# Eight heads in one row: reordering the steps of the later attentions in a fused fp32 transformer kernel

## The reference

```python
h = shift_token(x)                       # half of the columns come from the token before
q, k, v = split(h @ wqkv)                # 8 heads, 64 wide
q = l2norm(q) * qs; k = l2norm(k) * ksc
q, k = rotary_xpos(q, k)
# windows of 128 queries see their own 128 keys and the 128 before
sim = bq @ bk.T;  attn = softmax(where(mask, -max, sim));  o = attn @ bv
x = x + o @ wo
h = layernorm(shift_token(x)) * lg + lb
a, g = split(h @ w1 + b1);  x = x + (a * gelu(g)) @ w2 + b2
```

## Time and profile before

| | us |
|---|---|
| median of 3 runs | 1907.88 |
| lowest, highest | 1906.34, 1909.03 |
| the profiled execution | 1905.08 |
| its span in the trace | 1903.4 |
| PE busy | 1822.6 (96%) |
| DVE busy | 1580.5 (83%) |
| ACT busy | 1190.0 (63%) |
| POOL busy | 1090.9 (57%) |
| the two later attentions | about 625 to 1058 and 1268 to 1700 |

### The profile page before, as it was taken

One profiled execution on the slowest core, in us unless ns is written; L12 is line 12 of the kernel. 1 busy time (PEld: TensorE's weight loads), 2 busy tenths in 40 slices (PEclk: granted clock), 3 DMA queues, 4 the chain that ended last, 5 costly groups with the idle time before them and its releaser, 6 DMA issues. The chain is left out here.

```text
span 1903.4 us, 43278 instructions
## 1 busy us (share of the span) xinstructions
PE 1822.6 (96%) x15168; PEld 1529.0 (80%) x15168; DVE 1580.5 (83%) x3853; ACT 1190.0 (63%) x3084; POOL 1090.9 (57%) x1040
## 2 busy tenths in 40 slices
PE   6999999989999899999999999989999999989997
PEld 4777777768998788888887888878888888878886
DVE  6888888877988899999998566779999999966776
ACT  5787777764445577777776433347777777753332
POOL 3555444443434677777765355457777777634443
PEclk9999999999999999999999999989999999999999
DMA  2110111003241211111112333231111111122221
GB/s 100 32 34 30 52 42 33 21 24 106 77 121 47 97 41 51 41 49 48 43 46 65 120 110 109 93 116 36 50 50 40 51 42 49 35 81 67 77 77 34
DMA packets 139667, 116.01 MB, mean 61 GB/s; under 512 B 10440, under 2 KB 138704, under 8 KB 138704
## 3 DMA queue, kind: packets, MB, share of 16 engines
q1 hardware_dynamic: 139472, 113.53, 19.4%
HBM read 75.74 MB, written 37.75 MB: 60 GB/s over the span
## 5 line engine op out<-in xcount | busy, mean ns | idle before, releaser
L1715 ACT ACTIVATE b_probs<-masked,neg_max 128x256 f32<-128x256 f32 (+1 forms) x512 | 249.9, 498 | 8.3 <-DVE neg_max L1257 8.2
L542 PE MATMUL psum<-wa_hi,b_h_hi 128*128 128x512 f32 (+1 forms) x576 | 234.9, 408 | 0.2
L1257 DVE CUSTOM_DVE_ANT_0 masked<-psum,mask 128x256 f32<-128x256 f32 (+1 forms) x512 | 182.2, 412 | 43.4 <-PE psum L818 34.4
L544 PE MATMUL psum<-wa_hi,b_h_lo 128*128 128x512 f32 (+1 forms) x576 | 215.3, 374 | 0.0
L543 PE MATMUL psum<-wa_lo,b_h_hi 128*128 128x512 f32 (+1 forms) x576 | 215.1, 373 | 0.0
L542 PE MATMUL psum<-g_h_hi,wm_hi 128*128 128x512 f32 (+1 forms) x480 | 190.4, 397 | 6.2 <-POOL g_h_lo L1978 4.6
L1926 POOL TENSOR_TENSOR g_in<-g_in,minus_half 128x16 f32<-128x16 f32 x64 | 188.9, 2952 | 0.4 <-DVE g_in L1217 0.4
L543 PE MATMUL psum<-g_h_lo,wm_hi 128*128 128x512 f32 (+1 forms) x480 | 188.9, 394 | 0.0
L544 PE MATMUL psum<-g_h_hi,wm_lo 128*128 128x512 f32 (+1 forms) x480 | 188.8, 393 | 0.0
L1808 ACT ACTIVATE gate<-psum,vec_b 128x512 f32<-128x512 f32 x96 | 66.0, 687 | 168.6 <-PE psum L544 168.4
L542 PE MATMUL psum<-wm_hi,u_hi 128*128 128x256 f32 x576 | 165.6, 287 | 0.1
(11 more groups left out here) (161 smaller groups left out, 5778.3 us busy)
## 6 DMA issues: line engine op xcount, KB each, us to landing
x_mid<-y_out SPq DMA_DIRECT2D x96, 128.0 KB, 1.7
rope_in<-in_rope SPq DMA_DIRECT2D x64, 128.0 KB, 2.2
x_res<-x_state SPq DMA_DIRECT2D x64, 128.0 KB, 2.2
g_in<-x_mid SPq DMA_DIRECT2D x32, 256.0 KB, 3.7
g_old<-x_state SPq DMA_DIRECT2D x16, 512.0 KB, 4.1
out_x<-g_fin SPq DMA_DIRECT2D x15, 512.0 KB, 3.0
w_raw<-in_w_mlp_b SPq DMA_DIRECT2D x2, 2154.0 KB, 9.2
x_in<-in_x SPq DMA_DIRECT2D x32, 128.0 KB, 2.1
```

The source lines that it names most:

```text
L542: nc.tensor.matmul(out, a_hi, b_hi, start=first, stop=False)
L544: return nc.tensor.matmul(out, a_lo, b_hi, start=False, stop=last)
L1257: ins = nc.vector.tensor_tensor_reduce(out[:, at], src[:, at], (mask if now else mask0)[:, at], -1.0, BIG, ALU.add, ALU.min, neg_max[:, r, ...
L1715: ins = nc.scalar.activation(out, src, ACT.Exp, bias=neg_max[:, r, k:k + 1], scale=-1.0, accum_out=row_sum[:, n % 2, 4 * r + k:4 * r + k + 1])
```

## The change

In the later attentions a step now handles a chunk as a whole. Scores of heads 0 to 3 go to banks 4 and 5, those of heads 4 to 7 to banks 6 and 7, one right after the other; then come both halves of the values of the chunk before, and its spread. The transposed probabilities go back into the banks of their own scores. The output projection leaves bank 1 for bank 4 (6 and 5 at two places near the end). The order on every engine is written anew, `invert_sums` and `widen_inverse` belong to the step of their own chunk, and the openings of the MLP behind are placed anew in the last steps. Counts and sizes of operations stay. The diff is cut to the new order and the waits; the old order is in the code above, and the smaller edits are the bank numbers that go with the new places.

```diff
-def b_spread(n):
-
-    return 4 if n == NCH - 1 else 1
+def b_out(n):
+
+    return {NCH - 3: 6, NCH - 1: 5}.get(n, 4)


...


 def b_steps():
...
+                if n > 3:
+                    pe.wait_ge(S["r_copied"], g0 + n - 3)
...
+                    pe.wait_ge(S["h_hi"], g0 + n + 1)
+                    pe.wait_ge(S["h_lo"], g0 + n + 1)
...
-                if n + r > 0:
-                    pe.wait_ge(S["max_ready"], i)
+                if n > 0:
+                    pe.wait_ge(S["pt_act"], i - 1)
+                    pe.wait_ge(S["pt_dve"], i - 1)
+                if n > 2 and r == 0:
+                    pe.wait_ge(S["y_ready"], g0 + n - 2)
...
-                        out = bank[4 + b][:, j * 256:j * 256 + 256].rearrange("p (a k) -> p a k", a=2)
+                        out = bank[4 + 2 * r + b][:, j * 256:j * 256 + 256].rearrange("p (a k) -> p a k", a=2)
...
-                if n + r > 0:
-                    pe.wait_ge(S["pt_act"], i)
-                    pe.wait_ge(S["pt_dve"], i)
+                if n == NCH - 1 and r == 1:
+                    pe.wait_ge(S["y_ready"], g0 + NCH - 2)
...
-                        mm = nc.tensor.transpose(bank[6 + k // 2][:, at:at + P], b_probs[:, r, k, half, :], ident[:])
+                        mm = nc.tensor.transpose(bank[4 + 2 * r + k // 2][:, at:at + P], b_probs[:, r, k, half, :], ident[:])
...
                 pe.wait_ge(S["inv_wide"], g0 + n + 1)
-                pe.wait_ge(S["h_lo"], g0 + min(n + 5, NCH))
+                pe.wait_ge(S["v_copied"], g0 + min(n + 3, NCH))
                 if n == NCH - 1:
+                    pe.wait_ge(S["r_copied"], g0 + n)
+                for t in range(4):
+                    mm = nc.tensor.transpose(W2[:, t * P:t * P + P], b_inv_wide[:, t * P:t * P + P], ident[:])
+                mm.then_inc(S["inv_spread"], 1)
+
+            def out_project(n):
+                if n == NCH - 3:
                     pe.wait_ge(S["max_ready"], 2 * (g0 + NCH))
-                elif n > 0:
-                    pe.wait_ge(S["y_ready"], g0 + n)
-                out = bank[b_spread(n)]
-                for t in range(4):
-                    mm = nc.tensor.transpose(out[:, t * P:t * P + P], b_inv_wide[:, t * P:t * P + P], ident[:])
-                mm.then_inc(S["inv_spread"], 1)
-
-            def out_project(n):
-                pe.wait_ge(S["h_lo"], g0 + min(n + 6, NCH))
-                pe.wait_ge(S["v_copied"], g0 + min(n + 4, NCH))
+                elif n == NCH - 1:
+                    pe.wait_ge(S["pt_dve"], 2 * (g0 + NCH) - 1)
+                else:
+                    pe.wait_ge(S["pt_act"], 2 * (g0 + min(n + 2, NCH - 1)) + 1)
                 pe.wait_ge(S["o_hi"], g0 + n + 1)
                 pe.wait_ge(S["o_lo"], g0 + n + 1)
                 for k in range(c.KO):
-                    mm = product3(W2[:, 0:D], b_o_hi[:, k * P:k * P + P], b_o_lo[:, k * P:k * P + P],
+                    mm = product3(bank[b_out(n)][:, 0:D], b_o_hi[:, k * P:k * P + P], b_o_lo[:, k * P:k * P + P],
                                   wo_hi[:, k, :], wo_lo[:, k, :], k == 0, k == c.KO - 1)
...
+            for s in b_steps():
                 if b_chunk(s):
-                    scores(s, r)
...
+                    scores(s, 0)
+                    scores(s, 1)
+                if b_chunk(s - 1):
+                    values(s - 1, 0)
+                    values(s - 1, 1)
                     spread_inverse(s - 1)
...
+                if s == NCH:
+                    pe_mlp(pe, MLP_B, MB, layer, opening=0)
+                if s == NCH + 1:
+                    pe.wait_ge(S["pt_act"], 2 * (g0 + NCH))
+                    pe.wait_ge(S["pt_dve"], 2 * (g0 + NCH))
+                    pe_mlp(pe, MLP_B, MB, layer, opening=1)
+                if s == NCH - 1:
+                    out_project(s - 2)
+                if b_chunk(s + 2) and s + 2 > 1:
+                    project_k(s + 2)
+                if b_chunk(s):
+                    transpose_probs(s, 0)
+                if b_chunk(s + 2) and s + 2 > 1:
+                    project_q(s + 2)
+                if b_chunk(s + 3) and s + 3 > 1:
+                    transpose_x(s + 3)
+                if s == NCH - 1:
                     pe.wait_ge(S["kt_copied"], g0 + NCH)
                     pe.wait_ge(S["qt_copied"], g0 + NCH)
                     pe_mlp(pe, MLP_B, MB, layer, opening="z")
-                if (s, r) == (NCH, 1):
-                    pe_mlp(pe, MLP_B, MB, layer, opening=0)
-                if (s, r) == (NCH + 1, 0):
-                    pe.wait_ge(S["pt_act"], 2 * (g0 + NCH))
-                    pe.wait_ge(S["pt_dve"], 2 * (g0 + NCH))
-                    pe_mlp(pe, MLP_B, MB, layer, opening=1)
+                if b_chunk(s):
+                    transpose_probs(s, 1)
+                if b_chunk(s + 1):
+                    transpose_rotated(s + 1, 1)
+                    transpose_rotated(s + 1, 0)
+                if b_chunk(s - 2) and s != NCH - 1:
+                    out_project(s - 2)
+                if b_chunk(s + 2):
+                    project_v(s + 2)
...
+            for s in b_steps():
+                if s == NCH - 1:
+                    dve_mlp(v, MLP_B, MB, layer, opening=0)
+                if b_chunk(s):
+                    maxima(s, 0)
+                    maxima(s, 1)
+                if s == NCH - 1:
+                    dve_mlp(v, MLP_B, MB, layer, opening=1)
+                if b_chunk(s + 1) and s + 1 > 1:
+                    rotate_q(s + 1)
+                if b_chunk(s - 1):
+                    scale_o(s - 1)
+                if s == NCH - 1:
                     add_residual(s - 2)
...
+                    copy_probs(s, 0)
+                if s == NCH - 1:
+                    dve_mlp(v, MLP_B, MB, layer, opening=2)
+                if b_chunk(s + 1) and s + 1 > 0:
+                    scale_rotated(s + 1)
+                if s == 0:
+                    dve_mlp(v, *mlp_behind(layer), None if layer == 0 else layer - 1, opening="finish")
+                if b_chunk(s + 2) and s + 2 > 1:
+                    norms(s + 2, 1)
+                if b_chunk(s):
+                    copy_probs(s, 1)
+                if b_chunk(s + 2) and s + 2 > 1:
+                    norms(s + 2, 0)
+                if b_chunk(s):
+                    invert_sums(s)
+                if s == NCH - 1:
+                    dve_mlp(v, MLP_B, MB, layer, opening=3)
+                if b_chunk(s + 3) and s + 3 > 2:
+                    h_low(s + 3)
+                if b_chunk(s + 1):
+                    k_t_low(s + 1)
+                    q_t_low(s + 1)
+                if b_chunk(s - 2) and s != NCH - 1:
+                    add_residual(s - 2)
...
-                    if b_chunk(s - 1):
-                        copy_probs(s - 1, 1)
-                    if 4 <= s < 4 + 2 * SPLIT and s % 2 == 0:
-                        split_high(a, w_raw, wm_hi, wm_loaded, wm_hi_done, MLP_B.WCOLS, (s - 4) // 2, layer + 1)
-                else:
...
+            for s in b_steps():
+                if b_chunk(s + 1):
+                    copy_v(s + 1)
+                if b_chunk(s):
+                    exponentials(s, 0)
+                if b_chunk(s - 1):
+                    copy_spread(s - 1)
+                if b_chunk(s):
+                    exponentials(s, 1)
+                if b_chunk(s + 2) and s + 2 > 1:
+                    copy_qk(s + 2, 1)
+                    copy_qk(s + 2, 0)
+                if b_chunk(s):
+                    copy_probs(s, 0)
+                if b_chunk(s + 3) and s + 3 > 1:
+                    h_high(s + 3)
+                if b_chunk(s):
+                    copy_probs(s, 1)
+                if b_chunk(s + 1):
+                    k_t_high(s + 1)
+                    q_t_high(s + 1)
+                if s == NCH - 1:
+                    act_mlp(a, MLP_B, MB, layer, opening=True)
+                if b_chunk(s - 1):
+                    o_high(s - 1)
+                if 4 <= s < 4 + 2 * SPLIT and s % 2 == 0:
+                    split_high(a, w_raw, wm_hi, wm_loaded, wm_hi_done, MLP_B.WCOLS, (s - 4) // 2, layer + 1)
...
-                        tables(s + 2)
-                    if 4 <= s < 4 + 2 * SPLIT and s % 2 == 0:
-                        split_low(pool, nc.gpsimd, w_raw, wm_lo, wm_hi, wm_hi_done, wm_split, MLP_B.WCOLS, (s - 4) // 2, layer + 1)
-                    if b_chunk(s + 2) and s + 2 > 1:
-                        rotate_k(s + 2)
...
+                if b_chunk(s - 2):
+                    o_low(s - 2)
+                if s == NCH - 1:
+                    pool_mlp(pool, MLP_B, MB, layer, opening=0)
+                if s == NCH:
+                    pool_mlp(pool, MLP_B, MB, layer, opening=1)
+                if b_chunk(s + 1) and s + 1 > 1:
+                    inverse_norms(s + 1)
+                if b_chunk(s + 2) and s + 2 > 1:
+                    tables(s + 2)
+                if 4 <= s < 4 + 2 * SPLIT and s % 2 == 0:
```

(5 more changed lines are left out.)

123 lines of the change are left out of this document (11 added, 112 removed).

## The result

The changed kernel takes 1966.13 us (median of 4 runs, 1965.09 to 1967.71) against 1907.11 (1904.71 to 1909.03) for the kernel before: ratio 1.0311, 95% interval 1.0293 to 1.0329, **59 us slower**. I had forecast 1951. The profiled execution took 1967.71 us with a span of 1966.0, which is 62.6 more than the span of before. Where they went shows in the view of busy time by stretch. The borders are PE's first scores product of chunk 0, 4, 20 and 30, the first product of the MLP, and chunk 0 of the next layer. Columns: stretch, its length, busy PE, PEld, DVE, ACT, POOL, PEclk, DMA share, GB/s.

The account below looks back on a forecast made before the run. PE was taken to set the 13.2 us period, DVE 1 us behind. Per layer -4.3 plain chunks, +28.8 pairs, -0.8 chunk 16, +2.3 start, -4.5 end: +21.5, +43 for two layers, median 1951 us, range 1918 to 1974.

Parts of the forecast that it names:

- the mechanism named: Even steps 4 to 18: POOL's split_low, ahead of rotate_k and widen_inverse, waits 5 to 6 us for ACT's now last split_high.
- The pairs: Even step with a weight piece plus the next odd step: 30.0 instead of 26.4 us, +3.6, 8 pairs per layer, +28.8.
- The odd step: Step after a weight piece, from 12.8 to 30.0: PE waits for the widened inverse, DVE later for the inverse norms.
- The 1.3 for rotate_q's meetings with POOL: Odd step: rotate_q on DVE meets POOL's rotate_k, widen and o_low; +1.3 us, between 0 and 1.6.
- Plain chunk: Chunks without a weight piece: 12.85 us, PE bound at 12.8 with DVE at 12.7; -0.36 each, 12 per layer, -4.3.
- The end: From scores(30, 0) to the first MLP product, 29.8 us before: about -4.5 per layer, bounds -7 and 0.
- The start: First steps of a layer lose overlap, PE waiting for DVE's whole step: +2.3 per layer, bounds 0 and 4.
- The reciprocal's price: Reciprocal of the sums on DVE, now beside POOL's rotate_k: between nothing and 0.7 us per chunk, taken as nothing.
- Rival 1: POOL's slack swallows the wait for split_high, all chunks bound by PE: 1882 us in all, chance 0.10.
- Rival 2: No rotate_q meeting, tables not in the way, ACT one slot earlier: 27.6 per pair, 1912 us, chance 0.10.
- rival 3: DVE bounds plain chunks, through the reciprocal or a tensor_scalar held by rotate_k: 13.4 instead of 12.85, 1964 us, chance 0.14.
- Rival 4: POOL's power operation blocks rotate_q in plain chunks: 12 lose 1.4 us each, +34, 1985 us, chance 0.02.

Follow-up runs that it names:

- experiment 1: Changed kernel with ScalarE's weight piece (split_high) at the head of its step, behind copy_v, instead of last: 1903.86 us, 0.9985 of the kernel before.
- experiment 2: Changed kernel with POOL's split_low behind widen_inverse instead of ahead of rotate_k, split_high left last on ScalarE: 1891.66 us, 0.9919 of the kernel before.
- experiment 3: Kernel before the change, old order, with only split_high moved to the end of ScalarE's second half step: 2032.19 us, ratio 1.0659.
- experiment 9: Kernel of experiment 8 with VectorE's scaling of the values done twice in every chunk: 1913.89 us, 1.0026 of the kernel before.
- Experiment 4: Changed kernel with the MLP's first loads issued ahead of the store of chunk 28 on SyncE: 1957.39 us, 1.0265 of the kernel before.
- experiment 8: Changed kernel with split_low behind widen_inverse, MLP loads ahead of chunk 28's store, and MLP statistics behind chunk 31's maxima: 1873.53 us, 0.9832 of the kernel before.

## Why the prediction was right or wrong

- **Slower, in the range, by the mechanism named.** POOL waits 47.4 us for wm_hi, 8 times, longest 6.4 (forecast 5 to 6 each); the widenings alternate between 12.2 and 17.6. The pairs cost +28.8 in the first layer's stretch and +26.8 in the second's, where the forecast had 28.8 - 0.8 = 28.0. Experiments 1, 2 and 3 show the cause from both sides: two ways to take the wait away give back 62 and 74.5 us, and the late piece alone makes the old kernel 126 us slower.
- **The odd step: the right length, in part by luck.** From 757.30 to 774.48 it takes 17.2 us, as forecast (30.0 - 12.8), but by other parts. The stretch behind PE's wait, with the columns of the first view, and VectorE's next two operations:

```profile
763.80:767.12 3.32, 3.32 (x11) 2.75 (x12) 2.46 (x3) 2.17 (x8) 3.32 (x2) 0.53 0.00 0
```

```profile
768.19 0.69 DVE L1363 COPY b_pt<-psum 128x512 f32<-128x512 f32 x1 [1.89 <-PE psum L839]
...
768.80 1.53 DVE L1240 TENSOR_TENSOR g_in<-g_in 128x512 f32<-128x512 f32 x2
```

The 4.6 us over a plain step are 3.0 at the spread (forecast 2.2), 1.4 in the spread and the K projection behind it, which PE did at a granted clock of 0.53 (0.77 and 2.55 us instead of 0.42 and 1.48), and 0.25 where scale_rotated met POOL's tables (1.53 instead of 1.28). The forecast let the inverse norms come last. They were there at 768.47, and VectorE still worked on the copy of probabilities, for which it had stood 1.89 us waiting for PE; only in two of the eight pairs did it wait for the norms (2.1 us in all). The lower clock had no term in the forecast. The 1.3 for rotate_q's meetings with POOL are there (its addition at 764.05 takes 1.64 instead of 0.69), but they end as the spread's copy arrives, for which VectorE had to wait anyway. Both chains ended within 0.3 us of each other, so that by an estimate from these rows full clock alone would give back only these 0.3.

- **Plain chunk: right sign, undersized.** Forecast 12.85 (-0.36), measured 12.56 (-0.64). PE's parts on its timeline: two score groups 1.62 (936.50 to 938.12, forecast 1.59), both values groups 1.90 (to 940.02, forecast 2.06), spread 0.42 (to 940.44, forecast 0.49), V projection into scores 1.48 (947.58 to 949.06, forecast 1.57). With these and smaller differences in the rest the sum of 12.8 was 0.24 too long, and 0.05 were added for nothing in case VectorE came close. The claim that VectorE is 0.1 us below PE was right: experiment 9 measures 0.14 to 0.2. VectorE's loop is thus 12.3 to 12.4, not the 12.7 that I worked out; both loops were overestimated by nearly the same.
- **The end: wrong sign, the step that failed.** The forecast said about -4.5 per layer, "with one round per chunk instead of two", and "SP's queue is unchanged". The queue's order is unchanged, but its store of chunk 28 waits for a residual add that the change moves to the end of VectorE's step, and the loads stand behind it. And VectorE's statistics, which stood behind a first group of maxima, stand ahead of all of them. Measured +5.9 and +3.5 in the two layers, and +2.0 and +1.9 behind the border, where two output projections now lie instead of one. Experiment 4 takes 6.3 of the first layer's end away, experiment 8 8.6, and then it is shorter than before the change. The granted clock has a share in it that no run separates: the same 229 matmul records kept PE busy for 22.96 us at 0.86, and for 20.05 at 1.00.
- **The number** was 15 short, mostly for this reason. For the profiled execution the forecast was +43 and the result +62.6. Both ends together are 18.3 above the forecast and the stretches behind them 3.8; the larger gain of the ten plain chunks takes 5.5 back, and the rest are small terms. This makes 19.6; the medians show 15, since the profiled execution after the change was 1.6 above its median, and I had counted with 2.8 below.
- **The start:** +2.2 and +3.6 against +2.3.
- **The reciprocal's price** is nothing: 186/196/199 ns as shortest, median and longest of 64. The Trainium skill (SBUF — State Buffer, "Who interferes with whom") does not list it among those that take the shared port; the trace agrees.
- **Rival 1** (1882) named what would be had without the wait; experiment 2 with 1891.66 comes near it. Its ends are 35.6 and 33.9 us, 18 more than forecast, and its shorter plain chunks take a part of that back. As a forecast it was wrong: ACT's piece came at the place in its queue that I gave. **Rival 2** (27.6 per pair) and **rival 3** (13.4 per plain chunk) are refuted by 29.7 and 12.56. **Rival 4** is refuted: VectorE's product at 940.28 ran undisturbed under POOL's power, and the plain chunk has no 1.4 us more.

## What to carry to other kernels

When an engine gets a new order, look for the instruction that becomes last, and at every queue in which somebody waits for it: the waiting instruction's own place decides what stands behind it. Moving the consumer behind what others need (experiment 2) gave more than moving the producer forward (experiment 1), because it also chose whom it meets: maxima, and not scale_rotated. A DMA queue counts even if its order is untouched: ask what its waits now wait for. And idle time that always stands at the same place in a loop may be latency of that loop; doubling one operation shows in one run whether it is free.
